# Attention and feed-forward block: first q and k rows by TensorE picks, epilogue and projections one step on

## What is computed

```python
x = x + _layernorm(_L0_attn_ref(_layernorm(x, axis=-1), Wq, Wk, Wv, Wo), axis=-1)
x = x + _layernorm(_L0_ffn_ref(_layernorm(x, axis=-1), weight, alpha, bias), axis=-1)
# in _L0_attn_ref
q = _rope(x @ Wq); k = _rope(repeat(x @ Wk)); v = repeat(x @ Wv)
p = jax.nn.softmax(jnp.einsum('bhqd,bhkd->bhqk', q, k) / jnp.sqrt(256.), axis=-1)
return jnp.einsum('bhqk,bhkd->bhqd', p, v) @ Wo
# in _L0_ffn_ref
w_ternary = where(w > delta, 1, where(w < -delta, -1, 0)); delta = 0.7 * mean(abs(w))
out = einsum('bsd,od->bso', input, w_ternary * alpha) + bias
```

## Time and profile before

| | us |
|---|---|
| median of 3 runs | 1465.2 |
| lowest and highest run | 1464.79, 1470.04 |
| the profiled execution's own time | 1462.74 |
| its span, first to last instruction | 1460.9 |
| start to the first row maximum on DVE | 44.94 |
| first row maximum to the first exponential on ACT (72.86) | 27.9 |
| mean granted PE clock | 0.981 |

### The profile page before, as it was taken

How to read it: one execution, slowest core, us unless ns; L and a number is a source line. 1 busy time by engine, 2 the same in 40 slices (tenths; PEclk the granted TensorE clock), 3 DMA queues, 4 the chain that set the end, 5 groups by cost and what they waited for, 6 DMA issues and landing times.

```text
span 1460.9 us, 33107 instructions
## 1 busy us (share of the span) xinstructions
PE 1407.0 (96%) x12800; PEld 439.8 (30%) x12800; DVE 1325.6 (91%) x1478; ACT 1241.7 (85%) x2470; POOL 750.4 (51%) x1203
## 2 busy tenths in 40 slices
PE   6799999999999999999999999999999999999996
PEld 5122223222232223322232222322233222222235
DVE  5798999999999999999999999999999999999915
ACT  2089999898998989898998989999998989989881
POOL 3323274655665475745656555744756454363240
PEclk9589999999999999999999999999999999999999
DMA  4311131311312130221313122221301122120000
GB/s 146 89 27 53 29 73 42 103 31 51 71 62 67 50 85 24 89 53 47 77 40 99 31 72 50 75 66 45 78 31 60 46 60 69 37 67 32 32 27 30
DMA packets 72546, 84.58 MB, mean 58 GB/s; under 512 B 17444, under 2 KB 58276, under 8 KB 70948
## 3 DMA queue, kind: packets, MB, share of 16 engines
q1 hardware_dynamic: 71444, 81.46, 20.1%
q10 hardware_dynamic: 944, 0.98, 0.2%
HBM read 46.40 MB, written 24.63 MB: 49 GB/s over the span
## 4 chain that ended last, share of the span: by engine, by line
PE 75%; ACT 10%; DVE 8%; issue 3%; POOL 2%; DMA 1%; SPq 0%; ACTq 0%; POOLq 0%; DVEq 0%
PE pv L1063 30%; PE smax L1041 29%; ACT probs L925 8%; DVE row_max L1357 6%; PE ring L1218 5%; PE ring L1180 3%; PE ring L1226 2%; PE ring L1097 2%; ACT heads L995 1%; PE ring L1210 1%; PE ring L1191 1%; PE ring L1141 1%; PE ring L1164 1%; ACT act L984 1%; ACT xT L899 0%
## 5 line engine op out<-in xcount | busy, mean ns | idle before, releaser
L1357 DVE TENSOR_REDUCE row_max<-smax 128x1 f32<-128x1024 f32 x1024 | 1197.8, 1215 | 73.1 <-PE smax L1041 65.4
L925 ACT ACTIVATE probs<-ring 128x512 f32<-128x512 f32 x2048 | 1102.3, 596 | 89.1 <-PE ring L1097 60.2
L1041 PE MATMUL smax<-k_rows,q_rows 48*128 48x512 f16 x2048 | 628.8, 388 | 12.7 <-DVE row_max L1357 7.3
L1063 PE MATMUL pv<-probs,v_cols 128*32 128x256 f32 (+1 forms) x7136 | 627.6, 424 | 10.9 <-ACT heads L995 10.9
L1097 PE MATMUL ring<-q_rows,k_rows 50*128 50x512 f16 x2048 | 628.5, 383 | 0.1
L1041 PEld LDWEIGHTS smax<-k_rows,q_rows 48*128 48x128 f16 x2048 | 114.1, 94 | 486.6 <-issue 243.9
L1063 PEld LDWEIGHTS pv<-probs,v_cols 128*32 128x32 f32 x7136 | 140.9, 108 | 356.7 <-issue 196.5
L1097 PEld LDWEIGHTS ring<-q_rows,k_rows 50*128 50x128 f16 x2048 | 128.7, 93 | 30.3 <-ACT probs L925 26.4
L589 POOL TENSOR_TENSOR attnT<-pairs,inv_rows 128x512 f32<-128x512 f32 x31 | 39.6, 1276 | 175.5 <-DMA inv_rows<-inv_sums_dram 175.5
L568 POOL TENSOR_TENSOR act<-act,bias_sb 128x256 f32<-128x256 f32 x60 | 42.5, 730 | 115.5 <-ACT act L984 115.5
L1218 PE MATMUL ring<-wo_sb,attnT 128*128 128x256 f32 x256 | 71.3, 403 | 1.7 <-POOL attnT L589 1.1
(11 more groups left out here) (177 smaller groups left out, 1071.2 us busy)
## 6 DMA issues: line engine op xcount, KB each, us to landing
q_stage_dram<-q_parts SPq DMA_DIRECT2D x45, 256.0 KB, 2.5
q_rows<-q_stage_dram SPq DMA_DIRECT2D x30, 384.0 KB, 5.5
res<-in_L_attn_x SPq DMA_DIRECT2D x16, 512.0 KB, 4.1
pairs<-heads SPq DMA_DIRECT2D x63, 128.0 KB
inv_rows<-inv_sums_dram SPq DMA_DIRECT2D x31, 256.0 KB
out<-res SPq DMA_DIRECT2D x15, 512.0 KB, 3.4
x_in<-in_L_attn_x SPq DMA_DIRECT2D x7, 1024.0 KB, 6.6
k_rows<-k_stage_dram SPq DMA_DIRECT2D x64, 96.0 KB, 3.3
```

Source lines behind the costliest of these rows:

```text
L925: eng.activation(probs[:, s % PSLOTS, j, :], ring[:, (h.base + n) % RING, :], ACT.Exp, scale=score_unit).then_inc(ring_read, 1)
L1041: mm = eng.matmul(smax[:, side, c, :], q_rows[at:to, qc, kv * KVP + jp, qt * P:(qt + 1) * P], k_rows[at:to, kv, c * 512:(c + 1) * 512], st ...
L1063: mm = eng.matmul(pv[j * VCOLS:(j + 1) * VCOLS, cols], v_cols[:, g, kt, :], probs[:, s % PSLOTS, j, cols], start=(kt == 0 and first == 0), ...
L1357: eng.tensor_reduce(row_max[:, g % 2, at:at + 1], smax[:, side, :, :].rearrange("p c n -> p (c n)"), AX.X, ALU.max).then_inc(max_read, 1)
```

## The change

1. The epilogue is one step behind in every half (`behind`), the projections of q and k stand one step later (15, 16, 30 become 16, 17, 31), SP's store moves from step 3 to 6, its x load from 6 to 8, its residual load from 10 to 11. `X_NORM` stays at 18 and `F_NORM` at 31.
2. The start: k's swap is done by four DVE copies (`swap_first_k`). POOL builds two sets of picking matrices out of the identity (`make_picks`), PE multiplies the split k and q tiles with them into `smax` (`key_rows`, `query_rows`), ACT copies the result into `k_rows` and `q_rows`. The other key groups and q rows still go through DRAM, now with q staged by SP. The second half's q projections are two jobs of 512 columns in place of four of 256.
3. `pick_rows` is made at the start.

```diff
 PRO = {2: [("XT", 0, 0)], 3: [("XT", 1, 0)], 4: [("XT", 0, 1)], 5: [("XT", 1, 1)],
-       15: [("Q", 0, 0)], 16: [("K",)], 30: [("Q", 0, 1)]}
-
-PRO1 = {5: [("VT",)], 7: [("VN",)], 16: [("Q", 1, 0)], 30: [("Q", 1, 1)]}
+       16: [("Q", 0, 0)], 17: [("K",)], 31: [("Q", 0, 1)]}
+PRO1 = {5: [("VT",)], 7: [("VN",)], 17: [("Q", 1, 0)], 31: [("Q", 1, 1)]}
 PRO1_ALONE = {21: [("V", 0), ("V", 1)], 22: [("V", 2), ("V", 3)], 23: [("WT",)],
-              25: [("Q", 1, 0, 0)], 26: [("Q", 1, 0, 1)], 27: [("Q", 1, 1, 0)], 28: [("Q", 1, 1, 1)]}
+              25: [("Q", 1, 0)], 26: [("Q", 1, 1)]}
...
 ACT_SPLIT, BIAS = {21: 0, 23: 1}, {26: (0, 1), 28: (2, 3)}
-X_LOAD_FIRST, X_LOAD, STORE, RES_LOAD = 15, 6, 3, 10
+X_LOAD_FIRST, X_LOAD, STORE, RES_LOAD = 15, 8, 6, 11
 K_ROT, Q_ROT_FIRST, Q_ROT = 28, 22, 8
...
 XT_TILES = 2
+KEY_ROWS, QUERY_ROWS = 24, 29
 ROOM = {"Q": 2, "K": 2, "VT": 3, "WO": 1, "FF": 1}
...
         self.very_first = scores and not flush
-        self.behind = 1 if scores and epi is not None and pro is None and pro1 is None else 0
+        self.behind = 1 if scores and epi is not None else 0
         self.last = self.alone and epi is not None
...
         inv_fold = wq_in[:, 1, :]
+        pick_q = probs[:, 2, 0, :].bitcast(F16).rearrange("p (s e b m) -> p s e b m", s=KVP, e=2, b=2)
+        pick_k = probs[:, 2, 1, 0:HALF // 2].bitcast(F16).rearrange("p (a b m) -> p a b m", a=2, b=2)
...
         rot_other = sem("rot_other")
-        q_first = sem("q_first")
+        picks_made = sem("picks_made")
+        rows_full = sem("rows_full")
+        q_made = sem("q_made")
         parts_step = sem("parts_step")
...
-                eng.wait_ge(ring_read, h.done("K", 1) if h.alone else h.done("K"))
+                eng.wait_ge(ring_read, h.done("K"))
                 for tile in range(4):
...
                         take_k(h.b + 1, s // KT - 1)
-                    if h.pro is not None and s == K_SWAP:
+                    if h.pro is not None and not h.alone and s == K_SWAP:
                         swap_k(h)
...
                 if h.alone and h.pro is not None:
+                    stage_q(0, 0)
                     eng.wait_ge(consts, CONSTS)
-                    take_k(0, 0)
-                    load_other_q()
                     for g in range(1, HKV):
                         take_k(0, g)
+                    load_other_q()
                 elif h.pro1 is not None and not h.scores:
...
+            def make_picks():
+                eng.memset(pick_q, 0.0).then_inc(picks_made, 1)
+                eng.memset(pick_k, 0.0).then_inc(picks_made, 1)
+                eng.wait_ge(picks_made, 2)
+                q_cols = ident_h[:, :].rearrange("p (i r h) -> p h r i", i=NPAIR, r=2)[:, 0:KVP]
+                k_cols = ident_h[:, :].rearrange("p (a d h) -> p a h d", a=2, d=HD)[:, :, 0]
+                for blk in range(NBLK):
+                    for e in range(2):
+                        at = blk * HD + e * NPAIR
+                        eng.tensor_copy(pick_q.rearrange("p s e b (r m) -> p s e b r m", r=2)
+                                        [:, :, e, QPARTS[blk], :, at:at + NPAIR], q_cols).then_inc(picks_made, 1)
+                    for side in range(2):
+                        at = side * SIDE + blk * HD
+                        eng.tensor_copy(pick_k[:, :, KPARTS[blk], at:at + HD], k_cols).then_inc(picks_made, 1)
+                eng.wait_ge(w_cols, 6 * DT)
+                eng.tensor_copy(pick_rows, ident[:, :].rearrange("p (c j r) -> p c j r", c=ST, j=G)[:, :, :, 0:1]
+                                .broadcast_to([P, ST, G, HD])).then_inc(pick_made, 1)
             def take_v(h, b, g):
...
                 for s in h.steps:
-                    if h.last and s == 0:
-                        eng.wait_ge(w_parted, 2)
-                        eng.tensor_copy(pick_rows, ident[:, :].rearrange("p (c j r) -> p c j r", c=ST, j=G)[:, :, :, 0:1]
-                                        .broadcast_to([P, ST, G, HD])).then_inc(pick_made, 1)
+                    if h.alone and h.pro is not None and s == h.x_norm + 1:
+                        make_picks()
                     if h.scores and h.flush and h.qc == 0 and s == 3:
...
-            def stage_first_q():
-
-                for blk, part in enumerate(QPARTS):
-                    eng.wait_ge(parts_step, split_at(0, "Q0") + 1 + part)
-                    eng.dma_start(q_dram[0, blk, :, :, :, :].rearrange("(e i) r h n -> (i r h) e n", e=2),
-                                  q_parts[:, part, :, 0, :]).then_inc(q_staged[0], 16)
-
-            def load_first_q():
+            def key_rows():
                 eng.wait_ge(consts, CONSTS)
-                eng.wait_ge(q_staged[0], 16 * NBLK)
-                for side in range(2):
-                    eng.dma_start(q_rows[side * SIDE:side * SIDE + KROWS, 0, 0:KVP, :],
-                                  q_dram[0, :, :, side, 0:KVP, :].rearrange("m d h n -> (m d) h n"))\
-                       .then_inc(q_first, 16)
+                for a in range(2):
+                    eng.wait_ge(rows_full, a + 1)
+                    for at in (0, SIDE):
+                        eng.activation(k_rows[at:at + KROWS, 0, a * HALF:(a + 1) * HALF],
+                                       smax[at:at + KROWS, 1, a, :], ACT.Copy).then_inc(k_loaded[0], 8)
+            def query_rows():
+                for slot in range(KVP):
+                    eng.wait_ge(rows_full, 2 + slot + 1)
+                    eng.activation(q_rows[0:SIDE + KROWS, 0, slot, :], smax[0:SIDE + KROWS, 0, slot, :], ACT.Copy)\
+                       .then_inc(q_made, 1)
...
                 for s in h.steps:
-                    if h.alone and h.pro is not None and s == 24:
-                        stage_first_q()
-                        load_first_q()
+                    if h.alone and h.pro is not None and s == KEY_ROWS:
+                        key_rows()
+                    if h.alone and h.pro is not None and s == QUERY_ROWS:
+                        query_rows()
                     if s % KT == LAG and ((s > LAG and h.scores) or (s == LAG and h.flush)):
...
                     else:
-                        eng.wait_ge(q_first, 16 * 2)
+                        eng.wait_ge(q_made, 1)
                     eng.wait_ge(k_loaded[kv], (row + 1) * 16 * 2)
+                if part == 0 and side == 0 and c == 0 and not h.scores and kv == 0:
+                    eng.wait_ge(q_made, 2)
...
                     parts = h.values_at(s) if (h.scores and s >= LAG) or (h.flush and s < LAG) else {}
+                    if h.alone and h.pro is not None and s == KEY_ROWS:
+                        key_rows()
+                    if h.alone and h.pro is not None and s == QUERY_ROWS:
+                        query_rows()
                     if h.last and s == 0:
...
                             n = projections(h, h.jobs_behind(s, i), n)
+            def key_rows():
+                eng.wait_ge(picks_made, 2 + 4 * NBLK)
+                eng.wait_ge(parts_step, split_at(0, "K") + 2)
+                for a in range(2):
+                    for part in range(2):
+                        mm = eng.matmul(smax[0:SIDE + KROWS, 1, a, :], pick_k[:, a, part, 0:SIDE + KROWS],
+                                        k_parts[:, part, :], start=(part == 0), stop=(part == 1))
+                    mm.then_inc(rows_full, 1)
+            def query_rows():
+                eng.wait_ge(parts_step, split_at(0, "Q0") + 2)
+                for slot in range(KVP):
+                    for part in range(2):
+                        for e in range(2):
+                            mm = eng.matmul(smax[0:SIDE + KROWS, 0, slot, :], pick_q[:, slot, e, part, 0:SIDE + KROWS],
+                                            q_parts[:, part, e, 0, :], start=(part + e == 0), stop=(part + e == 2))
+                    mm.then_inc(rows_full, 1)
...
                     elif kind == "Q" and h.alone:
-                        at = a[0] * HALF + a[2] * HALF // 2
+                        first, last = (a[2] * HALF // 2, (a[2] + 1) * HALF // 2) if a[2:] else (0, HALF)
+                        at = a[0] * HALF
                         for dt in range(DT):
-                            mm = eng.matmul(dst[:, 0:HALF // 2],
+                            mm = eng.matmul(dst[:, 0:last - first],
                                             wq_sb[:, dt, a[1], :, :, :].rearrange("p i r h -> p (i r h)"),
-                                            xT[:, dt, at:at + HALF // 2], start=(dt == 0), stop=(dt == DT - 1))
+                                            xT[:, dt, at + first:at + last], start=(dt == 0), stop=(dt == DT - 1))
                     elif kind == "Q":
...
+            def swap_first_k(h):
+                eng.wait_ge(ring_read, h.done("K", 1))
+                for tile in range(4):
+                    own, other = tile * NPAIR * HKV, (tile ^ 1) * NPAIR * HKV
```

(3 more changed lines are left out.)

## The result

| | before | after |
|---|---|---|
| median, us | 1465.3 | 1476.7 |
| lowest and highest of six runs | 1462.44, 1470.04 | 1472.97, 1477.35 |
| the profiled execution, its span | 1462.74, 1460.9 | 1477.31, 1475.5 |
| first row maximum on DVE | 44.94 | 38.09 |
| last step's scores to the end of the span | 44.7 | 41.7 |

After over before is 1.0075, with an interval of 1.0056 to 1.0093: 11.4 us slower by the medians. The forecast was 1462.5 with a range of 1449 to 1469, so it was wrong, in sign and in range.

The account below looks back on a forecast made before the run. The plain step was taken as held by ACT's four exponentials, with DVE level. The terms -10.5 - 2.8 - 1.1 - 2.1 + 13.8 = -2.7, from the median 1465.2, gave 1462.5 us, range 1449 to 1469.

Parts of the forecast that it names:

- A: Start, first rows of q and k by copies and picks: first maximum at 34.4 instead of 44.94, 10.5 us less.
- B: End, pick matrix made at the start: PE no longer waits for POOL's copy, clock stays; 2.8 us less, 1.5 to 2.8.
- C: Output product one step later: PE's waits for POOL's scaled heads are covered, 1.1 us less.
- D: Rest of epilogue and projections one step later: 0.16 less in each of 13 halves, 2.1 us less.
- E: POOL at step 18 of six halves: x's normalisation before y's makes y 2.4 late; 2.3 each, 13.8 us more.
- R4: Rival: picks give 6 instead of 10.5, POOL's copies slowing DVE or picks running one by one; 1467.0, chance 0.10.
- step 18: Step 18 now follows a projection step; no sign known, 2 us allowed either way.
- R1: Rival: y's normalisation is in time, so the gain comes without the bill; 16.5 us less, 1448.7, chance 0.12.
- R2: Rival: PE's clock stays full through the lead and first scores; 2.5 us less, 1460.0, chance 0.20.
- R3: Rival: POOL's attention normalisation comes over a step later in six halves; 23.4 us more, 1485.9, chance 0.05.

Follow-up runs that it names:

- y first: The changed kernel with y's four normalisations put back ahead of x's eight on POOL at step 18 of the odd halves; 1447.4 us, ratio 0.9882.
- picks late: The changed kernel, but POOL makes its picking matrices only once DVE has normalised x; 1472.8 us, ratio 1.0051.
- pause filled: The changed kernel with nine identity matmuls on PE ahead of its wait for y in the six odd halves; 1462.0 us, ratio 0.9986.

## Why the prediction was wrong

| part | forecast, us | measured in the profiled executions, us | from |
|---|---|---|---|
| A | -10.5 | -6.9 (-8.6 to -10.4 with a shorter fall or none) | first score |
| B | -2.8 | -3.0 | end |
| C and D | -3.2 | -3.3 | halves, y first |
| E | +13.8 | +26.8 | odd halves, after against y first |
| half 10 | 0 | +0.8 | a wait for a DMA, +0.6 in picks late, none in y first |
| sum | -2.7 | +14.4 | spans: +14.6 |

The medians are only 11.4 apart: the profiled execution of before lay 2.5 below its median, that of after 0.6 above.

**E, the term that failed.** The mechanism stood as written: x's eight normalisations between y's root and y's normalisation, in six halves, PE waiting for POOL and ACT for PE. So did the size of the wait: 2.4 forecast, 2.29 measured. Wrong is the step "so ACT loses 2.4 + 0.7 - 0.9 = 2.2, and a little until the score slots are filled again: 2.3 in each". It prices PE's work behind the pause at the full clock. Measured, the clock falls 1.5 to 1.8 us into the pause, to 1.2 GHz for 6.8 us, in five of six halves. PE is busy 8.80 of 8.80 us behind the fall even at the full clock, so at half of it the step of 2.2 cannot be held, and another 2.6 is lost: 4.8 to 4.9 in each of the five, 26.8 in all instead of 13.8. The run with the pause filled separates the two: same lateness, full clock, 2.3.

The rows for it were at hand. The earlier trace rows show a pause of 2.60 with the clock at 0.57 behind it, and part B credits 0.9 for the clock when that pause goes. The same reading, turned round, belonged to the pause of 2.4 that part E adds. It would have been a case to weigh and no certainty, since the start of the same trace has a pause of 2.34 ahead of 15.23 and the clock is 1.00 until 35. With E at twice its price the sum is -2.7 + 13 = +10, 1475, close to the time measured. "The prediction falls if E is absent or over 3 us" was the right bound, and the range did not reach to it: E's ends were 1.6 and 2.6.

**A, the start: direction right, 3.6 too much.** First maximum 38.09 instead of 34.4. Swap and picks cost what was said. R4's first half held: POOL's fills beside DVE's normalisation cost it 1.0 us, a term that part A left at nothing. Most of the rest is the clock, whose fall in the start costs 3.0 in the profiled execution of after (against 35.04 without a fall), 1.3 in others and nothing in two. With the fills out of the normalisation's way and the clock kept it is 34.66, and there a fill still costs DVE 0.65. R4 gave 6 instead of 10.5, and the profiled run gave 6.9, so for this part the rival was nearer; its other half, picks one by one, did not happen.

**B** came by the way told: no pause for POOL, clock kept.

**C and D** together were -3.2, and the kernel with y first has -3.3 in its halves. C: PE no longer waits for POOL's scaled heads. D: the two copies of the second product stand 5.36 apart instead of 5.51, as was put down, and step 18, for which no sign was given, went from 2.63 to 2.46. Hidden inside is a loss of 0.46 in step 29 of each even half, by DVE's hold, which was not forecast and which gains in other steps outweigh.

**R1** was E absent: 1448.7. The kernel with y first is that case, and gave 1447.4. That the two are so near is in part luck: in the profiled executions its parts sum to -14.8, since the start gave 8.6 and not 10.5. **R2** did not happen. The clock was 0.50 in the lead of every profiled execution of these kernels, from 3 to 4 us after the first maximum for 34.1 or 37.5 us. The row of after:

```profile
40.00:76.00 36.00, 31.46 (x97) 4.75 (x99) 35.00 (x34) 8.06 (x16) 9.46 (x10) 0.53 0.23 65
```

As the prediction held, taking the long pause out ahead of the lead did not keep the clock up in it. **R3** did not happen: half 3 begins 2.5 earlier in after (322.4) than in the frame of part E (324.9), and x's join starts at 366.51, which is 369.0 in that frame, where 369.0 was put down.

**Open.** Why the sixth pause, as long as the others, has no fall. It was the same in picks late: six pauses of 2.29 or 2.30, a fall in the first five and none in half 11. In both kernels half 10 is longer by 0.8 or 0.6, so this pause comes that much later after the one before it than the others do; whether it hangs on that, no run tells. Why pauses of nearly the same length at other places have no fall is open as well. Nor was it tried to take the hold at step 29 away altogether.

## What to carry to other kernels

Price a new wait of TensorE in two parts: its length less what its consumers have in store, and the work behind it at half the clock. If a row of the kernel has a pause of that size with a low clock behind it, the second part belongs into the sum, or at least into the range. When a table moves a stage by one step, list for each engine which stages now share a step with it and in which order the code issues them. What did not move (here `X_NORM`, `K_ROT`) is where the new conflicts are. Where a pause can't be removed, cheap matmuls into a free buffer can keep the clock, as nine of them did here.

## What the runs showed of the hardware

- **A pause of 2.3 us in a saturated stretch dropped TensorE's clock** from 2.4 to 1.2 GHz in ten of twelve cases (after and picks late, five of six in each), 1.5 to 2.1 us into the pause, for 6.8 us, though PE is busy 6.24 of those in half 3 of after; a pause of 1.31 to 1.34 did so in none of six. At the start pauses of 2.31 to 2.33 went without a fall four times and one of 2.69 once (picks late, ahead of 9.84), those of 2.83 to 3.51 had one each, of 3.4 or 6.8 us. So between 2.3 and 2.7 us it went either way here. (The Trainium skill, "TensorE: Matmul & The Clock Gate", Part 1, says that activity releases the throttle and an idle stretch restores it, and that the point of the change varies from run to run; the trace agrees, and picks late has its start and its halves on both sides.)
- **Small DVE instructions are held by a GpSimd instruction until it ends:** 0.17 us became 0.93 and 0.53, each ending within 0.03 us of POOL's two-input operation. (The Trainium skill, "SBUF — State Buffer", Who interferes with whom, says that a VectorE instruction with two SBUF inputs contends with a GpSimd instruction that reads SBUF, and that the shared ports are an exclusive lock; by that a hold lasts to the end of POOL's instruction, and both do.) The same was seen with one input beside POOL's fill: 128x2 in 0.92 instead of 0.17, and eight normalisations in 3.67 instead of 2.68. (The same section of the Trainium skill allows this for such an instruction in a two-port mode; no run here shows the mode.)
- **Maxima of the lead did not hold the clock up.** From 3 to 4 us after the first of them it was 1.2 GHz in all eight new kernels, for 34.1 or 37.5 us, whatever the pause ahead had been.
